# A vision-transformer block on one core: scores from one head stacked twice in a row tile, and q and k projected sooner

## The reference, cut to what matters

```python
x_proj = silu(layernorm(h) @ W1 + b1)
u, v, q, k = split(x_proj, 4)                  # 16 heads of 16 columns each
scores = einsum('bqhd,bkhd->bhqk', qh, kh)     # per head, no softmax
attn = silu(scores) / S
av = einsum('bhqk,bkhd->bqhd', attn, vh)
y = layernorm(av * u, gamma, beta) @ W2 + b2   # h = h + y, then the experts
```

## Time and profile before

| what | value |
|---|---|
| median of 3 runs | 1768.78 us (1766.21 to 1779.12) |
| the profiled execution | 1769.26 us, its span 1767.4 us |
| TensorE matmul busy | 1430.8 us, 81% |
| VectorE busy | 1128.1 us, 64% |
| ScalarE busy | 928.5 us, 53% |
| GpSimd busy | 462.6 us, 26% |
| mean granted clock of TensorE | 0.894 |

### The profile page before, as it was taken

The page is one execution under the profiler, slowest core; times in us unless marked ns, Lnnn a source line. Parts: engine busy times, 40 slices in busy tenths (PEclk is TensorE's granted clock), DMA queues, the critical chain, the costliest instruction groups (busy, mean ns, idle before and its releaser), DMA issues. The chain is left out here.

```text
span 1767.4 us, 35208 instructions
## 1 busy us (share of the span) xinstructions
PE 1430.8 (81%) x12545; PEld 1159.3 (66%) x12545; DVE 1128.1 (64%) x3026; ACT 928.5 (53%) x1620; POOL 462.6 (26%) x372
## 2 busy tenths in 40 slices
PE   2499999999999999999986223204699999999997
PEld 1267667767667666767755222204699999999996
DVE  3255665665565565666653776786577777777774
ACT  0276766766666666766652035411455555555552
POOL 0011111221121121221210000016355555555553
PEclk8699999999999999999995555556799999999999
DMA  3533343343243342442113130000365655566652
GB/s 118 127 101 99 83 117 99 80 119 102 77 119 96 83 119 67 112 118 77 40 34 115 75 2 0 0 0 1 119 177 176 173 158 158 172 178 175 175 135 40
DMA packets 128691, 177.37 MB, mean 100 GB/s; under 512 B 19966, under 2 KB 116996, under 8 KB 124484
## 3 DMA queue, kind: packets, MB, share of 16 engines
q1 hardware_dynamic: 111172, 154.49, 29.7%
q0 software_dynamic: 17408, 21.25, 7.4%
HBM read 134.28 MB, written 41.41 MB: 99 GB/s over the span
## 5 line engine op out<-in xcount | busy, mean ns | idle before, releaser
L612 ACT ACTIVATE at<-ps_s 128x1024 f32<-128x1024 f32 x256 | 248.8, 1027 | 39.6 <-PE ps_s L499 37.1
L195 PE MATMUL ps_s<-xet,whi 128*128 128x322 f32 x640 | 207.1, 324 | 17.9 <-issue 11.0
L1702 POOL DMA_INDIRECT out_rows<-ye,slot_token x96 | 151.2, 1575 | 227.6 <-ACT ye L1560 213.2
L196 PE MATMUL ps_s<-xet,wlo 128*128 128x322 f32 x640 | 201.2, 314 | 0.0
L197 PE MATMUL ps_s<-xet,whi 128*128 128x322 f32 x640 | 200.0, 312 | 0.0
L1529 ACT ACTIVATE sg<-ps_s 128x322 f32<-128x322 f32 x160 | 70.6, 441 | 171.1 <-PE ps_s L197 148.4
L1624 DVE TENSOR_TENSOR wlo<-raw,whi 128x640 fp32r<-128x640 f32 x192 | 156.8, 817 | 1.3 <-ACT whi L1539 1.3
L499 PE MATMUL ps_s<-q,k 32*128 32x256 f32 x2048 | 148.8, 405 | 0.0
L195 PEld LDWEIGHTS ps_s<-xet,whi 128*128 128x128 f32 x640 | 122.4, 191 | 26.0 <-issue 26.0
L195 PE MATMUL ps_av<-whi,hs 128*128 128x256 f32 (+1 forms) x480 | 134.5, 280 | 2.9 <-DVE wlo L1624 2.9
L516 PE MATMUL ps_av<-at,uv 128*16 128x257 f32 x2048 | 136.0, 383 | 0.0
(11 more groups left out here) (343 smaller groups left out, 3655.3 us busy)
## 6 DMA issues: line engine op xcount, KB each, us to landing
raw<-in_wexp SPq DMA_DIRECT2D x32, 1280.0 KB, 6.2
halo<-gray_dram SPq DMA_DIRECT2D x96, 288.0 KB
xb<-in_x SPq DMA_DIRECT2D x64, 384.0 KB, 4.7
raw<-in_wexp SPq DMA_DIRECT2D x32, 640.0 KB
gray_dram<-g SPq DMA_DIRECT2D x32, 256.0 KB, 3.2
out_rows<-h SPq DMA_DIRECT2D x64, 128.0 KB, 6.3
token_rows<-xf SPq DMA_DIRECT2D x64, 128.0 KB, 3.5
pre_dram<-pre SPq DMA_DIRECT2D x32, 128.0 KB, 5.1
```

The source lines that it names most:

```text
L195: nc.tensor.matmul(o, lh, rh, start=first, stop=False)
L196: nc.tensor.matmul(o, ll, rh, start=False, stop=False)
L612: nc.scalar.activation(at[:, t, 2 * i:2 * i + 2, :, 0:R].rearrange("p j k q -> p (j k) q"), ps_s[i][:, :, :, :].rearrange("p j k q -> p (j ...
L1702: nc.gpsimd.indirect_dma_start(out=out, out_offset=bass.IndirectOffsetOnAxis(ap=slot_token[0:w, 3 * m + st:3 * m + st + 1], axis=0), in_=y ...
```

## The change

Queries and keys are now stored otherwise. ScalarE writes `qn` and `kn` once, with no zeroed copy. VectorE then copies each by a shuffle between partitions, within each 32, so that a row tile holds the even head twice (`dup[:, 0]`) or the odd one twice (`dup[:, 1]`). Of the keys the upper 16 rows keep the rounded value and the lower 16 the rest (`stack_k`; CUP is 0 or -1 by row). Of the queries the high part (`hi_q`, ScalarE) and the low part (`split_q`, VectorE) are stored apart. A score is then two products in f32r over 32 rows, one with each part of the queries, in place of one in f32. `cls_scores` uses `qn` and `kn`. The single buffers `qn`, `kn`, `dup` bring waits (q_dup, k_dup, cls_ps).

The order changes too: q's projection (B1) stands before `back`, k's (B2) before `router_pre`, and both silus stand together on ScalarE. `UNITS` follows, and with it the pairs of uses that share a bank.

```diff
-        UNITS = ["B0", "A0", "E", "D0", "D1", "G0", "B1", "D2", "A1", "D3", "B2", "B3", "B4", "D4"]
+        UNITS = ["B0", "A0", "E", "B1", "D0", "D1", "G0", "B2", "D2", "A1", "D3", "B3", "B4", "D4"]
...
             def cls_scores(n, r, m):
                 bank_free(pe, n, "E")
+                pe.wait_ge(qk_act, 2 * m + 2)
...
-                        for e in range(2):
-                            last = nc.tensor.matmul(mine[:, a, kt], k2[r % 2][:, e, a, kt * 128:kt * 128 + 128], qc[:, a, :],
-                                                    start=e == 0, stop=e == 1)
+                        last = nc.tensor.matmul(mine[:, a, kt], kn[:, a, kt * 128:kt * 128 + 128], qc[:, a, :], start=True, stop=True)
...
                 for kt in range(2):
-                    for j in range(4):
-                        last = nc.tensor.matmul(ps_s[j // 2][:, j % 2, kt, :], k2[r % 2][32 * j:32 * j + 32, e, a, kt * 128:kt * 128 + 128],
-                                                q2[r % 2][32 * j:32 * j + 32, a, :], start=True, stop=True)
+                    for hl in range(2):
+                        for j in range(4):
+                            row = slice(32 * j, 32 * j + 32)
+                            last = nc.tensor.matmul(ps_s[j // 2][:, j % 2, kt, :], kd[r % 2][row, e, a, kt * 128:kt * 128 + 128],
+                                                    qd[r % 2][row, hl, e, a, :], start=hl == 0, stop=hl == 1)
...
                 def silu_q():
                     act.wait_ge(qk_ps, 2 * b + 1)
+                    wait(act, q_dup, b)
+                    wait(act, cls_ps, b)
...
+                def hi_q():
+                    act.wait_ge(q_dup, b + 1)
+                    wait(act, scores, 4 * (b - 1))
+                    nc.scalar.activation(qd[(r + 1) % 2][:, 0, :, :, :].rearrange("p e t q -> p (e t q)"),
+                                         dup[:, :, :, :].rearrange("p e t q -> p (e t q)"), ACT.Copy).then_inc(q_hi, 1)
...
+                def shuffled(src, ready, done):
+                    dve.wait_ge(qk_act, ready)
+                    nc.vector.memset(spare[:, :], 0.0)
+                    for par in range(2):
+                        half = [16 * par + i for i in range(16)]
+                        last = nc.vector.stream_shuffle(dup[:, par, :, :].rearrange("p t q -> p (t q)"),
+                                                        src[:, :, :].rearrange("p t q -> p (t q)"), half + half)
+                    last.then_inc(done, 1)
...
+                def split_q():
+                    dve.wait_ge(q_hi, b + 1)
+                    nc.vector.tensor_tensor(qd[(r + 1) % 2][:, 1, :, :, :].rearrange("p e t q -> p (e t q)"),
+                                            dup[:, :, :, :].rearrange("p e t q -> p (e t q)"),
+                                            qd[(r + 1) % 2][:, 0, :, :, :].rearrange("p e t q -> p (e t q)").bitcast(f32),
+                                            ALU.subtract).then_inc(q_ready, 1)
...
+                def stack_k():
...
+                    dve.wait_ge(k_dup, b + 1)
+                    nc.vector.tensor_copy(flat_k, flat_d).then_inc(k_hi, 1)
+                    dve.wait_ge(k_hi, b + 1)
+                    nc.vector.scalar_tensor_tensor(flat_k, flat_k.bitcast(f32), cst[:, CUP:CUP + 1], flat_d,
+                                                   ALU.mult, ALU.add).then_inc(k_ready, 1)
```

More of the change, by code:

```diff
@@ L361, in build @@
         xt = s1("xt", [P, 2, 2, D], f32r)
-        q2 = [s1(f"q2{i}", [P, 2, D]) for i in range(2)]
-        k2 = [s1(f"k2{i}", [P, 2, 2, D]) for i in range(2)]
+        qn = s1("qn", [P, 2, D])
+        kn = s1("kn", [P, 2, D])
+        dup = s1("dup", [P, 2, 2, D])
+        qd = [s1(f"qd{i}", [P, 2, 2, 2, D], f32r) for i in range(2)]
+        kd = [s1(f"kd{i}", [P, 2, 2, D], f32r) for i in range(2)]
         uv_all = s1("uv", [P, 2, 2, 512])
@@ L481, in cls_scores @@
                 bank_free(pe, n, "E")
+                pe.wait_ge(qk_act, 2 * m + 2)
                 for a in range(2):
-                    nc.tensor.matmul(bank("E")[0:96, 0:256], kc[:, a, 0:96], q2[r % 2][:, a, :], start=a == 0, stop=a == 1)
+                    nc.tensor.matmul(bank("E")[0:96, 0:256], kc[:, a, 0:96], qn[:, a, :], start=a == 0, stop=a == 1)
                 mine = bank("E")[:, 256:288].rearrange("p (e a j k) -> p a k e j", e=2, a=2, j=4)
@@ L564, in body @@
                     score(n, r, c, 1)
+                if has(b):
+                    proj_qk(n, b, 0, "B1")
                 if has(d):
@@ L622, in silu_q @@
                     act.wait_ge(qk_ps, 2 * b + 1)
+                    wait(act, q_dup, b)
+                    wait(act, cls_ps, b)
                     for t in range(2):
[L624 removed]
+                        last = nc.scalar.activation(qn[:, t, :], bank("B1")[:, 256 * t:256 * t + 256], ACT.Silu,
                                                     bias=b1qk_sb[:, t:t + 1])
@@ L629, in silu_k @@
                     act.wait_ge(qk_ps, 2 * b + 2)
+                    wait(act, k_dup, b)
                     for t in range(2):
-                        for par in range(2):
-                            last = nc.scalar.activation(k2[(r + 1) % 2][:, par, t, :], bank("B2")[:, 256 * t:256 * t + 256], ACT.Silu,
-                                                        bias=bk4[:, 2 * par + t:2 * par + t + 1], scale=cst[:, CE2 + par:CE2 + par + 1])
+                        last = nc.scalar.activation(kn[:, t, :], bank("B2")[:, 256 * t:256 * t + 256], ACT.Silu,
+                                                    bias=b1qk_sb[:, 2 + t:3 + t])
                     last.then_inc(qk_act, 1)
+                def hi_q():
[3 more added lines that the diff above has]
+                                         dup[:, :, :, :].rearrange("p e t q -> p (e t q)"), ACT.Copy).then_inc(q_hi, 1)
                 def silu_uv(hf):
@@ L769, in body @@
                     nc.vector.tensor_copy(stt[0:NST, :], bank("G0")[0:NST, 256:512]).then_inc(stt_done, 1)
+                if has(b):
+                    wait(dve, k_ready, b)
+                    shuffled(qn, 2 * b + 1, q_dup)
                 if has(d):
@@ L786, in body @@
                     turned_lo(zt, bank("D2")[:, :], zt_hi, d, zt_done)
+                if has(b):
+                    split_q()
+                    dve.wait_ge(q_ready, b + 1)
+                    shuffled(kn, 2 * b + 2, k_dup)
+                    stack_k()
+                if has(d):
                     dve.wait_ge(w2_ps, d + 1)
```

25 lines of the change are left out of this document (12 added, 13 removed).

## The result

The changed kernel took 1941.28 us (median of 4, 1925.3 to 1944.7), the kernel before beside it 1772.83 (1766.21 to 1779.12): a ratio of 1.0933, 95% interval 1.0854 to 1.1012. It is slower by 168 us. The forecast was 1888, the range 1836 to 1962. The profiled execution is the quickest of the four, with a span of 1922.5 us at a mean granted clock of 0.869; in the other three the clock was 0.850 to 0.855.

What follows compares the result with a forecast made beforehand. TensorE was taken to set the 25.77 us step; after the change a ring through VectorE would, its terms summing to 29.8 us. 30 steps at +4.0 us add 120 to 1769: forecast 1888 us, range 1836 to 1962.

Steps and rivals of the forecast that it cites:

- ring: Image stage: dependency loop closing once per step through VectorE's in-order work, 22.08 us of work before, 29.8 us after.
- (a): From the start of VectorE's h2 add to the end of xt's low part: 10.85 us of work, unchanged.
- (b): From xt done on VectorE to TensorE's weight load of cls_scores: 0.16 us, unchanged.
- D1's wait: TensorE's second half of back waits for ScalarE's silu of q: some 1.6 us each step.
- rivals 2 and 3: VectorE's shuffles: fast, at 0.427 us, total 1857 us, chance 12%; slow, at half rate, 1970 us, chance 13%.
- Rival 4: TensorE's score row tiles don't run side by side: +1.05 us per step, 1920 us; chance 5%.
- TensorE's sum: TensorE's own work per image-stage step falls from 25.77 to 23.0 us.
- Clock still full: TensorE's clock in the image stage stays full, at a busy share of 7 or 8 tenths.
- Rival 5: TensorE's clock falls to 1.2 GHz for good: near 2200 us, outside the range; chance 4%.
- The fill ... at zero: The image stage's fill and last step, carrying only parts of the ring, add no time.
- the ring has 3.69 us to spare: In the kernel before, the ring's 22.08 us of work left 3.69 us of waits in the 25.77 us step.
- Rival 1: TensorE stays the bound at 23.0 us per step, so the change is faster: 1685 us; chance 4%.

Runs made afterwards that it cites:

- a_qfirst: The changed kernel with q's projection on TensorE and q's silu on ScalarE moved ahead of score pair 1: 1897.9 us, ratio 1.0725.
- a_copy: The changed kernel with plain copies of the same size in place of the four shuffles, so the output differs: 1910.0 us, ratio 1.0781.
- a_h0b: The changed kernel with GpSimd's addition h0b made to wait until VectorE's normalise xn is written: 1910.07 us, ratio 1.0781.
- a_warm: The changed kernel with 38 unused filler products a step on TensorE where it otherwise waits: 1917.06 us, ratio 1.0809.
- b_sooner: The kernel before, old storage, with only the changed order of q's and k's projections and silus: 1852.52 us, ratio 1.0452.
- s_pool: The kernel before with only the new storage, k's masked high part on ScalarE, its subtraction on GpSimd, h0b waiting for xn: 1844.75 us, ratio 1.0389.
- s_fix: s_pool with k's subtraction on VectorE behind the second biased tile and without h0b's wait: 1759.53 us, ratio 0.9897 against the kernel before.
- s_xt: s_fix with VectorE's statistics of xf issued behind xt's low part instead of ahead of it: 1727.48 us, ratio 0.9738 against the kernel before.
- a_mend: The changed kernel, order kept, with q ahead of score pair 1, q's shuffles later, h0b delayed, k's subtraction on GpSimd behind normalise z: 1818.72 us, ratio 1.0229.

## Why the prediction was right, and where its sizes were off

The sign and the mechanism held: the bound passed from TensorE's own sum to a ring that closes through VectorE's order. The terms, forecast against the step at 513.81 us:

| term | forecast | measured |
|---|---|---|
| (a) h2 add to xt's low part | 10.85 | 11.45 |
| (b) to the loads of cls_scores | 0.16 | 1.22 |
| (c) to the cls result | 1.87 | 1.93 |
| (d) to q's silu done | 4.34 | 4.05 |
| (e) D1 and the gated half | 1.16 | 1.17 |
| (f) to zt's low part | 6.97 | 6.79 |
| (g) k's block, to the h2 add | 4.42 | 4.53 |
| sum | 29.8 | 31.14 |

Point by point. **D1's wait** was forecast at some 1.6 us and was 1.61; a_qfirst took it away and gained 43 us. **z's turning** was to wait 1.2 us and waited 1.25. **The shuffle** was to take 0.7 us and took 0.73 to 0.74; rivals 2 and 3 fell with that, and a_copy shows that even a fast one leaves 1910 us. The estimate worked out from the Trainium skill, 0.79 us, was a little high. **The score groups** were to take 0.37 us less and took 0.40 less: 0.67 us from the start of a group to that of the next block (538.99 to 539.66), 1.07 before. Rival 4 fell. The Trainium skill ("TensorE: Matmul & The Clock Gate", "Wait — 56ns, not 53.3ns?") gives the 62 ns for each MATMUL only for a sequencer with hardware decode off. That would have made the group about 1.0 us. The trace has 16 products within 0.67 us, 42 ns each, so no such limit held here. **TensorE's sum** was put at 23.0 us and is 23.53 in the step at full clock. **h2** waits for TensorE no more.

What was off, +168 against +120:

- *(a), the step's work that was taken over unchanged.* The forecast let xn cost what it cost before. The forecast took the wait ahead of uvp out of (a), rightly; without it xn begins under h0b: +0.71 us a step, 0.60 in the term. a_h0b shows the cause, and gets 0.37 of it back, since its later h0b meets a copy.
- *"Clock still full".* It wasn't: 0.95 in this step and 0.93 in 100 to 500 us, where TensorE was busy 322.55 of 400 us (0.99 before, busy 388.06). The edge filter (L447) ran 1.93 us instead of 1.07 in front of cls_scores. In the steps at full clock (b) is 0.05 us, so all of its excess is the clock. Rival 5 had the clock falling for good or not at all; it fell for part of most steps, and a_warm prices that at 1.15 us in two of three. The other executions of the changed kernel had a clock lower still, and took 13 to 19 us longer than the profiled one; that the one comes from the other is likely, not shown.
- *"The fill ... at zero".* It costs 14.3 us: steps with only part of the ring are longer too.

At full clock and without the 0.7 the ring would be 29.98 - 0.7 = 29.3 us, a little under the forecast of 29.8; a_h0b has 29.6. The forecast step of +4.0 was 4.68.

That 1941 lies within the range owes something to luck. The upper end, 1962, was set for a slow shuffle, which didn't come; the 53 us above the forecast are the three terms above, none of which the upper end was made for.

One reading of the kernel before was wrong, though the sum doesn't suffer by it: "the ring has 3.69 us to spare". 2.44 of these are the end of TensorE's stretch from z's turning to the projection (b_sooner). The spare is 1.25 us. In the changed kernel k's block of 4.4 us takes the place of the 2.44, so 29.8 stands; but the order alone has 2.97 against 1.25, which is why b_sooner wasn't without cost.

The prediction's narrower claim, that the ring is what the order costs, needs b_sooner beside it. The order costs 80 us with the old storage, through D1's wait and the same late xn, which meet a ring with 1.25 us to spare. The storage alone, as first split over the engines, costs 70 (s_pool), and all of that and more went when k's subtraction left GpSimd and h0b's wait was dropped (s_fix, -85). Together they cost 168. Rival 1, that the change is a gain, was rightly small for this order. In another order, and with the statistics of xf moved, the new storage runs in 1727 us (s_xt).

Open stays why a_warm's step over the loop's end grew by 2.2 us; its granted clock was 0.86 there, as it was 0.85 without the filler.

## What to carry to other kernels

When an edit adds work to an in-order engine, sum the ring that closes through it, and put every wait that the edit creates at its place in that ring; then look which instructions of *other* engines will now run beside it, since a taken-over duration is only good in its old company. A wait that the engine has today is spare only if what it waits for doesn't itself follow from the ring. An edit's gain and its order are separate things: try the storage in the old order before giving the change up. A free engine is no free place: 1.2 us a step more on the busy VectorE, with h0b at its old time, was 85 us better than 2.4 us on the idle GpSimd.

## What the runs showed of the hardware

- A VectorE instruction can wait inside its own duration until a GpSimd tensor_tensor beside it has ended: a tensor_scalar of 256 elements 404 -> 1109 ns under h0b and 2226 ns under the subtraction of 1024; a copy and a multiplication of 2 elements 170 -> 1480 and 161 -> 1233 ns. The statistics of a norm (402 to 414 ns) and a sum that reads a bank (691 ns, 684 elsewhere) kept their times. The Trainium skill, "SBUF — State Buffer", section "SBUF: two separate sides", says that the two engines share a port pair as an exclusive lock, which the first one holds for its whole instruction, and names VectorE's two-port modes and operations with two SBUF inputs. The ends above, 0.02 to 0.16 us behind GpSimd's, agree. In a_mend the second kind shows: an addition of two tensors of 256 elements took 2.65 us instead of 0.42 (timeline below), in few of its steps, since its mean is 546 ns.

```profile
411.13 2.38 POOL L905 TENSOR_TENSOR kd<-dupk,kd 128x1024 fp32r<-128x1024 f32 x1 [8.48 <-ACT kd L652]
411.15 2.65 DVE L766 TENSOR_TENSOR h<-edge 128x256 f32<-128x256 f32 x1 [0.31 <-issue]
```

- TensorE's granted clock was 0.50 (1.2 GHz) from 523.04 to 526.45 us, behind waits of TensorE of 1.55 us (to 518.82) and 2.16 us (to 522.72), and the edge filter then took 1.93 instead of 1.07 us. Behind the same two waits one step earlier it stayed full.
- Row-tiled one-pass products of 256 columns go at 42 ns each, four row tiles at a time (16 within 0.67 us).
- The step over the end of the hardware loop took 4.1 us more than the others in the kernel before (2.8 to 5.0), 3.3 more than their mean in the changed one (34.0 against 30.8), and 6.2 with 38 products more in each step.
